# Two half tiles at the end of an expert loop, narrow tiles at regular places, and four smaller moves in an AdaLN + mixture-of-experts kernel

## The reference, cut to what matters

```python
# x: (4, 1024, 256); 8 experts, hidden 512, top 2
h = _layernorm(x) * (1 + ca) + sa
q, k, v = (unit_projection(h @ W.T + b) for W, b in ((Wq, bq), (Wk, bk), (Wv, bv)))   # each Fourier coefficient divided by its size
s = cumsum(bind(k, v), axis=1)                    # bind: product of the spectra
x = x + ga * unbind(s, q)
h = _layernorm(x) * (1 + cb) + sb
weights, sel = top_k(h @ gate_w, 2); weights = softmax(weights)
y_e = swiglu(h @ dense_1_w[e].T + b1[e]) @ dense_2_w[e].T + b2[e]     # for the two chosen experts of a token
x = x + gb * sum(weights * y_sel)
```

## Time and profile before

| | us |
|---|---|
| median of 3 runs (588.6, 591.45, 590.06) | 590.06 |
| the profiled execution, its own time | 588.21 |
| its span, first to last instruction | 586.1 |
| TensorE busy (share) | 543.3 (93%) |
| VectorE busy | 476.3 (81%) |
| ScalarE busy | 295.8 (50%) |
| GpSimd busy | 283.0 (48%) |

### The profile page before, as it was taken

One profiled execution on the slowest core, in us unless ns is written; L12 is line 12 of the kernel. 1 busy time (PEld: TensorE's weight loads), 2 busy tenths in 40 slices (PEclk: granted clock), 3 DMA queues, 4 the chain that ended last, 5 costly groups with the idle time before them and its releaser, 6 DMA issues.

```text
span 586.1 us, 13013 instructions
## 1 busy us (share of the span) xinstructions
PE 543.3 (93%) x3963; PEld 405.9 (69%) x3964; DVE 476.3 (81%) x1059; ACT 295.8 (50%) x501; POOL 283.0 (48%) x197
## 2 busy tenths in 40 slices
PE   8998999999999976688899999999999999999991
PEld 6544565555557443536588888888888888888870
DVE  1288889999999989979678888888888888888881
ACT  4776688878697863654333343333333333333330
POOL 0004033431523252000638877777877888887643
PEclk9998999989998996868999999999999999999997
DMA  8323644563745427724567797786786797867533
GB/s 309 128 97 108 192 123 130 160 162 109 215 108 158 132 90 248 294 40 74 150 131 102 126 150 120 141 149 113 135 149 115 134 143 146 139 134 120 78 41 36
DMA packets 82120, 79.52 MB, mean 136 GB/s; under 512 B 45140, under 2 KB 71892, under 8 KB 81816
## 3 DMA queue, kind: packets, MB, share of 16 engines
q0 software_dynamic: 16912, 31.74, 30.9%
q1 hardware_dynamic: 63864, 46.28, 30.0%
q10 hardware_dynamic: 1296, 0.87, 0.5%
HBM read 44.06 MB, written 22.23 MB: 113 GB/s over the span
## 4 chain that ended last, share of the span: by engine, by line
PE 63%; DVE 25%; issue 4%; ACT 3%; DMA 2%; POOL 2%; POOLq 0%; ACTq 0%; DVEq 0%
PE ps L798 31%; PE ps L817 15%; PE ps L545 7%; DVE region L1281 3%; POOL region L1702 2%; PE ps L604 1%; DVE region L1328 1%; PE ps L617 1%; DVE region L1425 1%; DMA out_rows<-w_stage,region 1%; DVE region L1296 1%; DVE region L1322 1%; DVE region L1323 1%; DVE region L1420 1%; DVE region L1245 1%
## 5 line engine op out<-in xcount | busy, mean ns | idle before, releaser
L798 PE MATMUL ps<-region,w_sb 128*128 128x256 f16 (+1 forms) x1872 | 195.0, 263 | 1.9 <-issue 1.0
L798 PEld LDWEIGHTS ps<-region,w_sb 128*128 x1872 | 170.3, 98 | 21.7 <-issue 2.8
L1733 POOL DMA_INDIRECT out_rows<-w_stage,region x71 | 125.2, 1763 | 59.3 <-DVE w_stage L1641 23.7
L1723 POOL DMA_INDIRECT region<-h_scratch,region x71 | 94.6, 1333 | 69.8 <-DVE region L1564 46.7
L1165 ACT ACTIVATE region<-region 128x1024 f16<-128x1024 f32 (+1 forms) x39 | 38.3, 982 | 129.0 <-DVE region L1617 129.0
L817 PE MATMUL ps<-region 128*128 x852 | 99.4, 273 | 2.0 <-DVE region L1623 1.7
L1609 DVE TENSOR_SCALAR region<-ps,region 128x256 f32<-128x256 f32 (+1 forms) x156 | 64.0, 456 | 45.2 <-PE ps L798 43.6
L817 PEld LDWEIGHTS ps<-region 128*128 128x128 f16 x852 | 82.7, 98 | 12.9 <-issue 3.2
L1153 ACT ACTIVATE region<-ps,region 128x256 f32<-128x256 f32 (+1 forms) x156 | 62.3, 450 | 56.1 <-PE ps L798 53.3
L545 PE MATMUL ps<-region 128*128 128x512 f32 x192 | 84.2, 595 | 3.2 <-ACT region L915 3.2
L1702 POOL TENSOR_TENSOR region<-region 128x512 f32<-128x512 f32 x30 | 37.2, 1266 | 96.3 <-DVE region L1308 96.3
(11 more groups left out here) (237 smaller groups left out, 704.5 us busy)
## 6 DMA issues: line engine op xcount, KB each, us to landing
w_stage<-in_w SPq DMA_DIRECT2D x20, 512.0 KB, 3.7
region<-in_x SPq DMA_DIRECT2D x8, 512.0 KB, 7.4
out_rows<-region SPq DMA_DIRECT2D x8, 512.0 KB, 3.0
h_scratch<-gb_bc SPq DMA_DIRECT2D x4, 1024.0 KB, 6.7
h_scratch<-region SPq DMA_DIRECT2D x8, 512.0 KB, 3.2
region<-region POOLq DMA_DIRECT2D x7, 512.0 KB, 4.5
region<-in_ramp SPq DMA_DIRECT2D x1, 2064.0 KB, 9.9
region<-in_w SPq DMA_DIRECT2D x4, 512.0 KB, 6.6
```

Source lines behind the costliest of these rows:

```text
L798: mm = pe.matmul(ps[:, GV + 2 * half + a, (f % 2) * MT:(f % 2) * MT + wide], w, xg_t[:, s, xa * KD + k, 0:wide], start=(n == 0), stop=(n = ...
L1723: G.indirect_dma_start(out=xg_rows[:, t % XG, u, :], out_offset=None, in_=h_scratch, in_offset=bass.IndirectOffsetOnAxis(ap=idx, axis=0)). ...
L1733: G.indirect_dma_start(out=out, out_offset=bass.IndirectOffsetOnAxis(ap=scatter_idx[:, at:at + 1], axis=0), in_=y_sb[:, t % 2, u, :], in_o ...
```

## The change

1. `gate_basis`: from block 2 on, the scaled basis is made before the block's products, behind `low_rows`.
2. Piece 0 of weight group 9 goes ahead of the gate matmuls of the last block but one, into a bank of its own; pieces 2 and 3 of group 11 go behind the transposes of the first expert tile, where three matmuls stood that only kept the clock up.
3. The one-hot tables are built in five steps, the last two of 8 columns.
4. The last wide tile becomes two halves (tiles 38 and 39, the same expert); the narrow tiles stand at 0, 6, 12, ..., 36. The loop then runs over tiles 6 to 35, and 36 to 39 are unrolled. The second half's scatter does not wait for that of the first.
5. In the unrolled tail only tile 39 is split (`low`) ahead of the rows of the tile before it; the rows of tile 36 are weighted ahead of the split of tile 37.
6. The word of tiles 0 to 6 is loaded once on each engine and handed on.

```diff
-MOE_TILES = BIG + SMALL
+MOE_TILES = BIG + SMALL + 1
-ROUNDS = BIG // XG
-NARROW = (0, 6, 12, 18, 24, 37, 38)
-FEW = NARROW.index(37)
-LOOPS = FEW - 1
+ROUNDS = (MOE_TILES - 2) // XG
+NARROW = tuple(range(0, MOE_TILES - 2, XG))
+HALVES = (MOE_TILES - 2, MOE_TILES - 1)
 def subs(t):
-    return 1 if t in NARROW else SUB
+    return 1 if t in NARROW + HALVES else SUB
+        STEPS = ((0, PC), (PC, 2 * PC), (2 * PC, 3 * PC), (3 * PC, 3 * PC + PC // 2), (3 * PC + PC // 2, PCOLS))
+        def low_bank(t, i):
+            return OUT if (t, i) == (9, 0) else TP + i % 2
...
             gate_rows(LAST - 1)
+            pe.wait_ge(l_x2, 1)
+            low_weights(9, (0,))
             gate(LAST - 1)
             for h in range(2):
                 last_rows(h)
                 last_gate(h)
-            low_weights(9, (0, 1))
+            low_weights(9, (1,))
             rank_totals()
             rank_all()
             low_weights(9, (2, 3))
             low_weights(10)
             place_pairs()
-            low_weights(11)
+            low_weights(11, (0, 1))
...
             first_rows(0)
-            keep_warm(3, ident_h[:], w1_sb[:, HI, 0:BLK], GV + 1)
+            low_weights(11, (2, 3))
             up(0, 0, e[0], None, between=lambda: first_rows(1), wide=P)
-            six_turns(0, first=True)
-            with pe.Fori(1, LOOPS) as n:
-                six_turns(n)
-            for t in range(XG * LOOPS, MOE_TILES):
+            six_turns(0, e, first=True)
+            with pe.Fori(1, ROUNDS) as n:
+                six_turns(n, experts(n))
+            for t in range(XG * ROUNDS, MOE_TILES):
...
-            for q in range(PARTS):
-                part = slice(q * PC, (q + 1) * PC)
+            for q, (at, to) in enumerate(STEPS):
+                part = slice(at, to)
...
-                ahead_of = t + 1 < MOE_TILES and t + 2 in NARROW + (MOE_TILES,)
+                ahead_of = t + 2 == MOE_TILES
                 if ahead_of:
                     low(t + 1, (t + 1) % 2, wide=P * subs(t + 1))
...
+            def gate_basis(b):
+                for r in range(2):
+                    ins = G.tensor_tensor(idft_ga[:, r, :], idft_sb[:, r, :], mod_bc[:, b, 0, :], ALU.mult)
+                ins.then_inc(ga_ready, 1)
             for t in range(NBLK):
                 s, b = t % 2, t // 2
                 if t >= 2:
                     pool.wait_ge(all_ready, t + 1)
                     low_rows(t - 2)
+                    if s == 0:
+                        pool.wait_ge(idft_done, t)
+                        gate_basis(b)
...
-                if u == 0 and t >= 1:
+                if u == 0 and t >= 1 and t != HALVES[1]:
                     pool.wait_ge(scattered[1 - t % 2], moved(t - 1, 2))
```

More of the change, by code:

```diff
@@ L825, in experts, with six_turns @@
                 return [word >> (3 * m) & 7 for m in range(XG + 1)]
-            def six_turns(n, first=False):
-                e = experts(n)
+            def six_turns(n, e, first=False):
                 for m in range(XG):
@@ L1184, in _ @@
             first_rows(0)
+            low_weights(11, (2, 3))
             gate_half(0, e[0], between=lambda: first_rows(1), wide=P)
             high(0, 0, wide=P)
-            six_turns(0)
-            with act.Fori(1, LOOPS) as n:
-                six_turns(n)
-            for t in range(XG * LOOPS, MOE_TILES - 1):
+            six_turns(0, e)
+            with act.Fori(1, ROUNDS) as n:
+                six_turns(n, experts(n))
+            for t in range(XG * ROUNDS, MOE_TILES - 1):
                 if t % XG == 0:
@@ L1666, in _ @@
             low(0, 0, wide=P)
-            six_turns(0, first=True)
-            with dve.Fori(1, LOOPS) as n:
-                six_turns(n)
-            for t in range(XG * LOOPS, MOE_TILES):
+            six_turns(0, e, first=True)
+            with dve.Fori(1, ROUNDS) as n:
+                six_turns(n, experts(n))
+            for t in range(XG * ROUNDS, MOE_TILES):
                 if t % XG == 0:
@@ L1703, in _ @@
                     ins.then_inc(x1_ready, 1)
[L1704 to L1712 removed]
+                if t == 0:
+                    pool.wait_ge(const_in, 48)
+                    pool.wait_ge(mod_in, 16)
+                    gate_basis(0)
             def gather(t, u):
```

42 lines of the change are left out of this document (17 added, 25 removed).

## The result

The changed kernel takes 586.45 us (median of 5 runs, 586.29 to 587.64) against 589.6 of the kernel before (5 runs, 588.6 to 591.45): ratio 0.9937, 95% interval 0.9914 to 0.9959, or 3.15 us less. The forecast was 7.4 less, and the result lies 0.45 us above the forecast's range. A second pair on another chip gave 0.9947 (0.9929 to 0.9964). The profiled execution took 586.35 with a span of 584.2, and the one of before 588.21 and 586.1.

The account below looks back on a forecast made before the run. It took TensorE and the drain's chain of scatters to bound the experts, VectorE's small operations the routing, VectorE the attention. Gains 0.5 + 2.1 + 4.75 = 7.35 us took 590.06 to 582.7; range 581.2 to 584.2.

Parts of the forecast that it names:

- The basis: Attention, blocks 2, 4 and 6: moving the scaled basis behind `low_rows` gains 0.5 us, bounds 0 and 2.5.
- the rival of the hidden basis: Attention: L1283 and L1286 pass before the basis, so the move gains 2.5 us instead of 0.5; chance 0.13.
- Low weights around the ranking: Routing: with one piece left behind the last gate, VectorE's ranking step L1483 comes 1.6 us earlier; bounds 0 and 1.98.
- five steps: Routing, one-hot tables: fewer last matmuls against an additional VectorE set, 0.1 us gained; bounds -0.3 and 0.4.
- Start of the experts: First gather to first wide `up`: earlier gather and one word load; 2.1 us gained for routing and start together.
- the rival of the clock: Start of the experts: TensorE at its lower clock over two pieces and first `up`, giving 2.1 us back; chance 0.17.
- the 0.99 us of the word: Start of the experts: dropping the second word load removes TensorE's 0.99 us before the first wide `up`.
- TensorE's work in the experts: Expert loop and tail: narrow tiles and the order of tile 36 make the last `up` end 1.0 us later.
- The 0.65 for the narrow tiles: Expert loop: two narrow `up` come in and one wide goes, 0.65 us more TensorE work.
- starved ring: Expert loop: narrow tiles make TensorE wait at tiles 30 and 36, costing 13.6 us; chance 0.03.
- The 0.35 for the order of tile 36: Unrolled tail: weighting tile 36 ahead of tile 37's split delays `down` of 37, taken as 0.35 us.
- The drain: Last scatters: tile 39's starts at about 575.5 and the span ends at 581.35, 4.75 us gained with TensorE's 1.0 counted in.

Follow-up runs that it names:

- the piece alone: Kernel before with only piece 0 of weight group 9 moved ahead of the gate matmuls: 588.94 us, ratio 0.9985.
- the whole last tile: Changed kernel with the last wide tile left whole, 39 tiles and no halves: 586.72 us, ratio 0.9943 to the kernel before.
- group 11 ahead: Changed kernel with pieces 2 and 3 of weight group 11 back ahead of the gather and three short matmuls back: 586.26 us, ratio 0.9934 to the kernel before.
- the word loaded twice: Changed kernel with the word of tiles 0 to 6 loaded a second time on each engine: 586.07 us, ratio 0.9937 to the kernel before.
- two targets: Changed kernel with odd tiles but 39 added to another tensor, no scatter waiting for a landing, those rows missing: 584.07 us, ratio 0.9903 to the kernel before.

## Why the prediction was right and wrong

*What bounds the kernel* held, stage by stage, with one omission: the chain of landings limits the tail from tile 35 on, and it was read only for the tiles 37 and 38.

*The basis* (forecast 0.5): right in direction, and the size was 0.6 to 0.8 in some traces and 1.9 in others. Among traces whose half-clock stretches fall at nearly the same places, the attention goes from 180.80 and 180.86 (before, and the piece alone) to 180.03 to 180.19 (four traces with the moved basis). In these, L1289 and L1292 grew by 0.32, 0.59 and about 0.46 us in blocks 2, 4 and 6, where 0.72 each had been worked out. Of the 2.5 us saved at L1328 and L1329, 1.4 were paid back there. In the first profile of the changed kernel `low_rows` starts 0.37 us behind the reciprocal in blocks 4 and 6, the two operations grew by 0.32, 0.13 and 0.13, and the attention took 178.58 in place of 180.44: 1.9 us, nearly the price of the rival of the hidden basis (2.5). It was hidden in part, by the earlier `low_rows` and not because VectorE's two operations passed before it. The Trainium skill's lock rule (SBUF — State Buffer, "SBUF: two separate sides") says that whichever starts first holds the shared pair for its whole instruction while the other waits. The traces agree in four places: each time the delay of VectorE's operation is what was left of GpSimd's product when it started, less 0.14 to 0.15 us (0.28 left and 0.13 paid in the first profile's block 4; 0.42 and 0.27, then 0.46 and 0.32, in the second's; 0.47 and 0.32 in block 2). In block 2, L1289 started first and took its 0.70, while the product beside it took 1.19 in place of 0.64.

*Low weights around the ranking* (1.6) and *five steps* (0.1): right in sum. It was 1.6 to 1.7 us in nine traces that have both or the first of them (47.43 to 47.55 against 49.16), 1.24 in the one taken with the result and 1.3 in that of the whole last tile.

*Start of the experts* (0.4 on top of the ranking): the step failed, in two places. The first is the rival of the clock, which had 0.17: the granted clock was 0.52 over most of the two pieces, and they took 3.85 us in place of 2.1. Against this rival the prediction had read that the clock "was back at 2.4 GHz as soon as these pieces ran". The trace of before shows otherwise: the first of the four pieces there began at 277.86, at a granted clock of 0.50 that lasted until 280.6, with L617 as long as at 254.37 (1.92):

```profile
277.86 1.98 PE L617 MATMUL ps<-region,ident_sw 128*128 128x512 f32 x2
```

So the first wide `up` came 0.6 us earlier relative to the attention's last products in the first pair (288.29 - 228.57 against 290.74 - 230.42) and 1.5 in the second (290.58 - 231.60 against 292.74 - 232.25), and not 2. The second was in no case: behind it stands `up` of tile 2, whose rows a DMA transposes, and this DMA is issued only when `up` of tile 0 has ended. Where `up` waited for it, it took 7.3 us or more from issue to reader. Before, `up` came 7.45 us behind the issue (289.84 + 7.45 = 297.29) without a wait, so hardly more than a tenth or two was to spare. With group 11 ahead the first wide `up` came 3.0 earlier on that scale (288.87 - 231.58), and `up` of tile 2 had 1.69 us of wait in front. So the 0.99 us of the word was priced at full and was worth nothing (the word loaded twice), and the clock was not worth its price either (group 11 ahead). Taking the DMA off tile 2, with group 11 ahead, gave 2.1 us by the medians and 0.8 by the traces.

*TensorE's work in the experts* (-1.0): -1.6. The 0.65 for the narrow tiles is about what is left without the wait below (1.6 - 0.90 = 0.7): rounds did not change, and there is no starved ring (43.52 of 43.70 busy). The 0.35 for the order of tile 36 was the wrong term: that order costs nothing (its split put back ahead, no difference). The 0.90 us before `down` of 37 comes from the placing of the narrow tiles, since a narrow `down` and a narrow `up` do not cover the activation of the wide tile 37.

*The drain* (5.75 with the last `up` as its start): this is the step that failed most, 3.3 us of it. "Behind VectorE's work on tile 37 its rows are ready near 562, and its scatter has landed at 562 + 1.56 + 2.97 = 566.5." The rows were ready at 561.12, but the scatter started at 565.16, since tile 35's two had begun at 557.16 and 559.14 and landed 3.7 us after their end. A wide tile takes 557.16 - 550.55 = 6.6 us in the chain, a narrow one 1.55 + 2.86 = 4.4. TensorE spends 2.84 + 0.18 + 1.47 = 4.5 on a narrow tile, so the chain cannot catch up there. And the rows of 35 were ready 4 us behind the start of 34's scatters, since the `up` between them is the narrow one of 36, where the chain needs 6.6. From there the delay is handed on: tile 36 has landed at 569.6 in place of 566.5, and tile 37, which starts then, at 576.3 in place of 573.0, where tile 38 starts. With the chain removed, the drain was 12.36 against 12.5 forecast. That the last scatters overlap and end 5.9 us after the start of the last was right (6.0), though they are 1.86 apart and not 0.3 to 1: tile 39's rows were there (576.26 + 0.52), and its scatter followed behind the late one of tile 38.

The rival that would have made it slower did not come, but it was near the cause: a narrow tile crowds the landings, and that shows in the drain and not in TensorE's rounds. (Among the chances, faster adds up to 0.92 by the prediction's own terms, not 0.91.)

Of gain, 4.2 us are missing. The landings are worth 2.7 (two targets) and tile 2's transposes up to 2.1. Without both, and with group 11 ahead, the kernel ran at 582.2, or 581.6 by its ratio. That is about where the forecast of 582.7 had put the change, but not proof of its terms: the attention gave more than forecast in that trace, and the start less.

What stays open: the medians differ by 3.0 to 3.15 us, each pair of traces by 1.9 to 2.1. The quicker attention that is told of below stands in five of the eleven traces with the moved basis and in none of the three without it. How often it comes in the runs behind the medians is not known, so whether it is the missing microsecond isn't either.

## What to carry to other kernels

When a chain of "wait for the previous landing" is shortened at its end, follow it back until a link waits for data and not for a landing; only from there on is the end a sum of durations. A transfer that lands just in time leaves no wait in the trace: before pricing a gain, take the time from the issue of every transfer to its first reader, and see which of them has no slack. And an edit that removes a visible stall is worth what the next wait leaves of it.

## What the runs showed of the hardware

**Where TensorE's clock falls differs from one trace to the next, and the stages' lengths differ with it.** The traces with their first product at 51.3 to 52.0 us and those with it at 49.8 to 50.0 differ in a stretch near 30 us. Busy time by stretch, of the kernel before in its second profile:

```profile
28.00:32.00 4.00, 4.00 (x21) 2.30 (x21) 1.76 (x1) 3.34 (x6) 0.00 (x0) 0.77 0.00 0
```

and the same program in its first:

```profile
28.00:32.00 4.00, 4.00 (x21) 2.05 (x21) 1.76 (x1) 3.34 (x6) 0.00 (x0) 1.00 0.00 0
```

Of the 1.5 us of difference at the first product about 1.0 arise there: eight matmuls of 512 columns (L508) take 5.29 us in place of 3.60, and VectorE's next chain (L1231) begins at 35.97 in place of 34.51, where the operation before it had been 0.45 apart. The attention differs too. In the changed kernel's second profile, near 180 us:

```profile
178.00:182.00 4.00, 4.00 (x33) 3.31 (x32) 3.96 (x11) 2.52 (x5) 1.64 (x2) 0.82 0.75 253
```

and in its first:

```profile
178.00:182.00 4.00, 3.84 (x50) 2.83 (x49) 3.90 (x29) 3.40 (x7) 4.00 (x4) 1.00 0.93 313
```

Where the clock is down near 180, the attention took 179.6 to 180.9 us (nine traces of all kernels); where it is up there and down near 204, 178.5 to 179.05 (five traces, all with the moved basis). From block 2 on, in both traces of the kernel before, the step from an even block's first product to the next block's took 26.3 to 26.5 us, and that from an odd one 25.3 to 25.5. With the moved basis every step from block 3 on is 25.4 to 25.5 us in the five quick traces. A granted clock of 0.57 from 129 to 133 us, in the changed kernel's second profile, goes with 26.5 us for the step there: the reciprocal came 0.6 later behind the block's first product (13.65 against 13.04), and `low_rows` another 0.7 later behind it, so that the basis met L1289 and L1292. So the moved basis was worth 1.9 us in the trace in which no such stretch falls there (178.58 against 180.44), and 0.6 to 0.8 in those with one near 129 and one near 180. Stages of two traces can be compared only where such stretches fall alike.

**A landing is not a constant.** Where a scatter waited for a landing, that came 2.9 to 3.1 us after the end of the issue; behind the issue of 2.31 us in the changed kernel it came after 3.7. Where TensorE waited for the transposing DMA of tile 2, it took between 7.3 and 9.8 us from issue to its reader, longest in the two-target kernel (288.00 to 297.77).
